# Moving VectorE's two-input chores, the key copy and the side products within each pair of heads

## What is computed

```python
x = x + attn_a(_layernorm(x), ...)
x = x + ffn(_layernorm(x), ...)
x = x + attn_b(_layernorm(x), Wq, Wk, Wv, Wo, gamma, beta)
x = x + ffn(_layernorm(x), ...)

# attn_b, its input called x
q = jnp.einsum('bsd,hde->bhse', x, Wq)      # k and v likewise
scores = jnp.einsum('bhse,bhte->bhst', q, k)
attn = softmax(where(causal, scores / sqrt(E), -inf))
out = jnp.einsum('bhst,bhte->bhse', attn, v)
y = x + heads @ Wo
y = (y - mu) * rsqrt(var + LN_EPS) * gamma + beta

# ffn: M = 64, INNER = 16
s = jnp.einsum('btd,dm->btm', x, Win) + bin_
h = relu(s[..., None] * W1 + b1)
g = jnp.einsum('btmh,mh->btm', h, W2) + b2
out = jnp.einsum('btm,md->btd', g, Wout) + bout
```

## Time and profile before

| | |
|---|---|
| median of 3 runs | 909.11 us (909.02 to 909.72) |
| the profiled execution | 910.46 us, its span 908.7 us |
| PE busy | 732.3 us (81%) |
| DVE busy | 740.5 us (81%) |
| ACT busy | 542.1 us (60%) |
| POOL busy | 522.9 us (58%) |
| heads | from about 239 us; the last pair's maxima at 864 us |

### The profile page before, as it was taken

The page is one execution under the profiler, slowest core; times in us unless marked ns, Lnnn a source line. Parts: engine busy times, 40 slices in busy tenths (PEclk is TensorE's granted clock), DMA queues, the critical chain, the costliest instruction groups (busy, mean ns, idle before and its releaser), DMA issues. The chain is left out here.

```text
span 908.7 us, 21242 instructions
## 1 busy us (share of the span) xinstructions
PE 732.3 (81%) x7592; PEld 524.5 (58%) x7592; DVE 740.5 (81%) x1422; ACT 542.1 (60%) x1511; POOL 522.9 (58%) x496
## 2 busy tenths in 40 slices
PE   3476666641899999998899899889989998998852
PEld 2365555531557676675677567666756665675541
DVE  1478888864577789889989988998898899899973
ACT  0357666652466665675677567666756666765643
POOL 2146666443165666756756575676658566656831
PEclk9598878855799999999999999999999999999995
DMA  9111110101199987897789688888878887887740
GB/s 202 42 32 42 50 56 35 36 35 46 21 144 155 155 141 132 140 149 124 127 138 152 108 141 132 142 131 138 151 117 131 144 139 125 136 154 126 133 93 22
DMA packets 367142, 100.29 MB, mean 110 GB/s; under 512 B 347968, under 2 KB 364864, under 8 KB 367040
## 3 DMA queue, kind: packets, MB, share of 16 engines
q1 hardware_dynamic: 363776, 96.86, 61.6%
q10 hardware_dynamic: 3264, 2.10, 0.9%
HBM read 8.73 MB, written 2.10 MB: 12 GB/s over the span
## 5 line engine op out<-in xcount | busy, mean ns | idle before, releaser
L1018 POOL TENSOR_TENSOR prob_hl<-prob,prob_hl 128x768 f16<-128x768 f32 (+1 forms) x192 | 347.8, 1812 | 235.6 <-DVE prob_hl L957 235.6
L933 ACT ACTIVATE prob<-wide,neg_max 128x128 f32<-128x128 f32 (+3 forms) x512 | 264.5, 525 | 209.1 <-DVE neg_max L969 209.0
L969 DVE TENSOR_REDUCE neg_max<-wide 128x2 f32<-128x256 f32 (+3 forms) x256 | 203.6, 816 | 66.5 <-PE wide L847 65.0
L842 PE MATMUL wide<-k_sb,q_sb 64*128 64x128 f32 (+3 forms) x1024 | 190.8, 470 | 2.6 <-ACT prob L933 1.6
L867 PE MATMUL bank<-v_hi,prob_t 128*128 128x64 f16 x1280 | 132.2, 193 | 16.6 <-DMA prob_t<-prob_hl 8.8
L869 PE MATMUL bank<-v_hi,prob_t 128*128 128x64 f16 x1280 | 132.2, 193 | 0.0
L868 PE MATMUL bank<-v_lo,prob_t 128*128 128x64 f16 x1280 | 132.2, 193 | 0.0
L957 DVE CAST prob_hl<-prob 128x768 f16<-128x768 f32 (+1 forms) x192 | 126.4, 658 | 1.8 <-ACT prob L933 1.6
L867 PEld LDWEIGHTS bank<-v_hi,prob_t 128*128 128x128 f16 x1280 | 115.5, 98 | 20.5 <-issue 10.6
L869 PEld LDWEIGHTS bank<-v_hi,prob_t 128*128 128x128 f16 x1280 | 114.0, 98 | 0.0
L868 PEld LDWEIGHTS bank<-v_lo,prob_t 128*128 128x128 f16 x1280 | 113.8, 98 | 0.0
(11 more groups left out here) (190 smaller groups left out, 1474.6 us busy)
## 6 DMA issues: line engine op xcount, KB each, us to landing
prob_t<-prob_hl SPq DMA_TRANSPOSE x384, 3.1
x_next<-in_L_attn_a_in_features SPq DMA_DIRECT2D x8, 256.0 KB, 3.1
x_attn<-in_L_attn_a_in_features SPq DMA_DIRECT2D x8, 256.0 KB, 3.0
x_sb<-x_done SPq DMA_DIRECT2D x8, 256.0 KB, 2.3
y_res<-bn_y SPq DMA_DIRECT2D x8, 256.0 KB, 2.3
out_x<-x_done SPq DMA_DIRECT2D x8, 256.0 KB, 2.7
wq_a<-in_L_attn_a_w_q ACTq DMA_DIRECT2D x1, 512.0 KB, 5.3
wq_b<-in_L_attn_b_Wq SPq DMA_DIRECT2D x1, 512.0 KB, 8.3
```

The lines of the kernel that those rows point to most:

```text
L842: pe.matmul(dst[:, h, c:c + m], q[e, i * P:(i + 1) * P], k[e, 0:m], start=(i == UNIT_ROWS[u][0]), stop=False)
L933: last = act.activation(prob_2[s][:, at:at + m], score_banks(p, s)[:, h, c:c + m], ACT.Exp, bias=neg_max[p % 2][:, h, i:i + 1], accum_out= ...
L969: last = dve.tensor_reduce(neg_max[p % 2][:, :, i:i + 1], score_banks(p, s)[:, :, c:c + m], AX.X, ALU.max, negate=True)
L1018: pool.tensor_tensor(prob_hl[u][:, w:2 * w], prob_2[u][:, 0:w], prob_hl[u][:, 0:w], ALU.subtract)\
```

## The change

Five moves, with the same arithmetic:

1. The key copy goes from DVE (s = 1, after the cast) to ACT (s = 1, after the `ctx_t` copy).
2. The adds go from s = 0 (behind `v_lo`) to s = 1, between the maxima and the cast of unit 0, one pair later; the relus go one pair later too.
3. Centering and residual are done in one piece of four instructions each, at s = 2 of pairs 3 and 4, between the maxima of unit 2 and the cast of unit 1.
4. POOL's and DVE's later chores follow by a step: `ffn_xb`, roots and the applied norm about two units later, statistics and moments one unit later.
5. PE's side products come last in a pair, behind `values_tensor`, and one pair later (turn in pair 7, Win in pair 0, Wout in pair 1; for sequence 6 one pair later in the drain). ACT's copies of their results move behind the exponentials and `v_hi`. There is one drain body more.

```diff
-        DRAIN = 2 * HP + 2
+        DRAIN = 2 * HP + 3
...
-        def unit_of_ffn(b, p, s):
-
-            if b == B:
-                return p * NU + s if p < NU else None
-            return p if s == 0 and 0 <= b - 2 < B else None
+        def relu_at(b, p, s):
+
+            if b == B and p > 0:
+                k = (p - 1) * NU + s
+                return (B - 2, k) if k < J else None
+            c, j = (b - 2, p - 1) if p > 0 else (b - 3, J - 1)
+            return (c, j) if s == 0 and 0 <= c < B and c != B - 2 else None
+
+        def adds_at(b, p, s):
+
+            found = []
+            c, j = (b - 2, p - 2) if p > 1 else (b - 3, J - 2 + p)
+            if s == 1 and 0 <= c < B and c != B - 2:
+                found.append((c, j))
+            k = (p - 1) * NU + s
+            if b == B and 0 < k <= J:
+                found.append((B - 2, k - 1))
+            return found
...
-        def keys_vector(dve, b, p):
+        def keys_scalar(act, b, p):
             n = number(b, p)
-            wait(dve, "k_ps", n + 1)
-            wait(dve, "s2", n - 1)
-            dve.tensor_copy(k_sb[p % 2][:, :], QK).then_inc(sem("k_sb"), 1)
+            wait(act, "k_ps", n + 1)
+            wait(act, "s2", n - 1)
+            act.copy(k_sb[p % 2][:, :], QK).then_inc(sem("k_sb"), 1)
...
-                if s == 2 and p == 6 and 0 <= b - 1 < B:
+                if s == 2 and b < B - 1:
+                    values_tensor(pe, b, p)
+                if s == 2 and p == 7 and 0 <= b - 1 < B:
                     back_turn_tensor(pe, b - 1)
-                if s == 2 and p == 7 and 0 <= b - 1 < B:
-                    back_s_tensor(pe, b - 1)
+                if s == 2 and p == 0 and 0 <= b - 2 < B:
+                    back_s_tensor(pe, b - 2)
                 if s == 2 and leaves(b, p) is not None:
                     back_out_tensor(pe, leaves(b, p))
-                if s == 2 and b < B - 1:
-                    values_tensor(pe, b, p)
...
+                for c, j in adds_at(b, p, s):
+                    back_add_vector(dve, c, j)
+                if s == 2 and p == 3 and 0 <= b - 1 < B:
+                    back_center_vector(dve, b - 1)
+                if s == 2 and p == 4 and 0 <= b - 1 < B:
+                    back_residual_vector(dve, b - 1)
                 u = (s - 1) % NU
                 if pair_exists(*(before if s == 0 else (b, p))):
                     split_vector(dve, *(before if s == 0 else (b, p)), u)
...
-                if s == 1 and pair_exists(*later(b, p)):
-                    keys_vector(dve, *later(b, p))
-                back_adds_vector(dve, b, p, s)
...
         def back_out_tensor(pe, c):
             wait(pe, "g_add", J * c + J)
+            wait(pe, "g_done", c)
```

More of the change, by code:

```diff
@@ L803, in project_tensor @@
             wait(pe, *(("k_sb", n) if done == "q_ps" else ("q_sb", n + 1)))
-            if done == "q_ps" and p == 0:
+            if done == "q_ps" and p == 1:
                 wait(pe, "g_xt", b - 1)
-            if done == "q_ps" and p == 1:
+            if done == "q_ps" and p == 2:
                 wait(pe, "g_s", b - 1)
-            if done == "q_ps" and p == 2:
+            if done == "q_ps" and p == 3:
                 wait(pe, "g_done", b - 2)
@@ L943, in heads_scalar @@
                     act.copy(ctx_t[:, :], MB[:, :]).then_inc(sem("ctx_t"), 1)
+                if s == 1 and pair_exists(*later(b, p)):
+                    keys_scalar(act, *later(b, p))
                 if s == 2 and b < B - 1:
                     values_scalar(act, b + 1, p, MB)
-                j = unit_of_ffn(b, p, s)
-                if j is not None and j < J:
-                    back_relu_scalar(act, b - 2, j)
+                if s == 2 and p == 7 and 0 <= b - 1 < B:
+                    back_xt_scalar(act, b - 1)
+                if s == 2 and p == 0 and 0 <= b - 2 < B:
+                    back_s_scalar(act, b - 2)
+                if relu_at(b, p, s) is not None:
+                    back_relu_scalar(act, *relu_at(b, p, s))
         def split_vector(dve, b, p, u):
@@ L1068, in back_rstd_gpsimd, with back_center_vector @@
                 .then_inc(sem(f"{done}_rstd"), 1)
-        def back_center_vector(dve, c, half):
+        def back_center_vector(dve, c):
             wait(dve, "gy_mv", c + 1)
-            for i in range(half * QB // 2, (half + 1) * QB // 2):
+            for i in range(QB):
                 last = dve.scalar_tensor_tensor(out=y_gb[:, i, :], in0=y_res[:, c * QB + i, :],
@@ L1076, in back_center_vector, with back_residual_vector @@
             last.then_inc(sem("g_c"), 1)
-        def back_residual_vector(dve, c, half):
-            wait(dve, "g_c", 2 * c + 2)
+        def back_residual_vector(dve, c):
+            wait(dve, "g_c", c + 1)
             wait(dve, "gy_rstd", c + 1)
             wait(dve, "x_beta", c + 1)
-            wait(dve, "g_xb", c)
-            for i in range(half * QB // 2, (half + 1) * QB // 2):
+            wait(dve, "g_y", 2 * c)
+            for i in range(QB):
                 last = dve.scalar_tensor_tensor(out=x_ffn[:, i, :], in0=y_gb[:, i, :],
@@ L1125, in back_gpsimd @@
                 wait(pool, "kept", 16 * B)
-                wait(pool, "g_x", 2 * c)
+                wait(pool, "g_x", c)
                 pool.tensor_tensor(x_beta[:, :, :], x_sb[:, seq(c), :],
@@ L1131, in back_gpsimd @@
                 back_rstd_gpsimd(pool, y_norm, "gy", c)
-            if p == 4 and u == 2:
-                wait(pool, "g_x", 2 * c + 2)
+            if p == 5 and u == 0:
+                wait(pool, "g_x", c + 1)
                 wait(pool, "g_done", c - 1)
@@ L1137, in back_gpsimd @@
                     .then_inc(sem("g_xb"), 1)
-            if p == 5 and u == 0:
+            if p == 5 and u == 2:
                 back_rstd_gpsimd(pool, ffn_norm, "gf", c)
@@ L1141, in back_gpsimd @@
                     .then_inc(sem("gf_nm"), 1)
-            if p == 5 and u > 0:
-                if u == 1:
+            if p == 6 and u < 2:
+                if u == 0:
                     wait(pool, "gf_rstd", c + 1)
@@ L1146, in back_gpsimd @@
                     wait(pool, "g_xt_ps", c)
-                for i in range((u - 1) * QB // 2, u * QB // 2):
+                for i in range(u * QB // 2, (u + 1) * QB // 2):
                     last = pool.tensor_scalar(ffn_norm.y[:, i, :], x_ffn[:, i, :], ffn_norm.neg_mean[:, i:i + 1],
@@ L1256, in _ @@
             queries_scalar(act, 0, 0)
+            keys_scalar(act, 0, 0)
             over_pairs(act, heads_scalar)
```

34 lines of the change are left out of this document (8 added, 26 removed).

## The result

The changed kernel takes 882.59 us in the median of four runs (878.94 to 884.83), the kernel before 909.07 beside it (908.64 to 909.72): ratio 0.9704, 95% interval 0.9671 to 0.9738, 26.5 us less. The prediction was 877. The profiled execution is the fastest of the four, 878.94 us, its span 877.1.

A forecast was written before the change was run, and what follows sets the result against it. PE sets the pace in bare heads; with chores it waits for DVE, held behind GpSimd's subtractions. Savings of 34.8 us less 3.0 in the drain, net 32 from profiled 910.46, less 1.35 to the median, gave 877 us; range 865 to 893.

The forecast's parts named there:

- PE as the new bound: Full sequences: DVE ceases to be the bound; 80.96 us falls to PE's floor of 73.75 plus 2.0, 75.75.
- The adds: At s = 1, behind unit 0's maxima: 0.74 us instead of 1.58, at least 0.84 saved a pair; pushed-back work has slack.
- key copy off DVE: -0.60 us a pair: Key copy moved to ACT in each pair: DVE saves 0.60 us, and ACT's copy costs 0.
- Pairs 3 to 7: Late casts of unit 2 delay `ctx_sb`; PE waits 0.1 us in pair 3, 0.3 to 0.4 in the others.
- late transposes hold PE a little everywhere: Rival: queueing transposes make PE wait 0.35 us in each of 56 pairs, 897 us; chance 12%.
- Centering and residual: Pairs 3 and 4, in one piece at t = 7.6: 1.2 us each instead of 3.6 and some 2.2.
- GpSimd's root holds them: Rival: in pair 3 centering stands still for two root instructions, 1.2 us later, 8.4 in seven sequences, 885 us; chance 7%.
- Sequence 7: Pair 0 to pair 7: transfers become the floor at 8.3 us a pair, 67.15 falls to 60.7, -6.4 us.
- The drain: Kernel's end: sequence 6's adds start later, 0.8 us of waiting and 2.2 for three more adds, 3.0 us given back.
- nothing happens: Rival: adds stand still in their new place too, pairs keep their pitch, 909 us; chance 3%.
- late transposes of unit 0 make it slower: Rival: unit 0's low half lands late, PE waits 1.2 us in 48 pairs, 58 us, 935 us; chance 3%.
- everything fits: Rival: no wait in pairs 3 to 7, 12 us less than the forecast, 865 us; chance 4%.

The follow-up runs named there:

- spread: Changed kernel with centering and residual as two instructions each at s = 1 and s = 2, GpSimd's applied norm one instruction a unit: 883.14 us, ratio 0.9706.
- light_low: Changed kernel, but from sequence 2 on a low half's transpose moves only two blocks, with as many transposes issued: 876.72 us, ratio 0.9637.
- second measurement: The changed kernel run once more, unedited, to see where its executions differ: 880.56 us, ratio 0.9676.

## Why the prediction was right, and where not

**PE as the new bound: right.** PE is busy for 74.70 of 75.80 us, before for 75.29 of 80.90. A full sequence takes 75.9 us in the mean of four; I gave 75.75. But what lies between it and the floor of 73.75 was right in size and wrong in place, as the paragraph on pairs 3 to 7 says; that the two sums agree to 0.2 us is in part luck. My sign "pitches of 8.9 to 9.5 in every pair" holds for pairs 2 to 6 only: those that hold a product took 10.18, 9.88 and 9.74.

**The adds: right.** 0.74 us each in the pairs of the row above, a mean of 0.849 over all 56, 1.563 before. Not every one is free of GpSimd: in pair 7 of four sequences the add takes 1.09 to 1.36, and in sequence 7, where PE leaves less room, one takes 1.69 (at 790.35, beside a subtraction of 789.35 to 791.49) and one 1.94; one of the drain takes 2.17. Slack was predicted for what they push back, and it held: no more than 1.1 us of PE's 75.80 is idle. The run with the adds put back gave 902.89 against an expected 902.

**Key copy: a term put down as DVE's saving that PE never sees.** The step "key copy off DVE: -0.60 us a pair" was true for DVE and nearly without effect, at most 2.6 us of 26 to 29. My sum did not rest on it, as it went by PE's floor; but my reading that ACT's copy costs nothing held only because other moves put the maxima on time. In the kernel before it costs 11 us.

**Pairs 3 to 7: the size right, the step wrong.** I had "`ctx_sb` then ends at about t = 3.7 of the next pair [...] So PE waits about 0.4 us". The casts of unit 2 do stand still (1.43 to 1.85 us), but PE's wait is for the landing of what they and the subtraction behind them deliver. I had worked out the slack of unit 0's low half only. The case in rows, pairs 6 and 7 of sequence 3: on DVE the late cast,

```profile
513.07 1.64 DVE L971 CAST prob_hl<-prob 128x1024 f16<-128x1024 f32 x1
```

on SP's queue the issue of its low half and of the next unit's high half,

```profile
517.01 1.23 SPq L1049 DMA_TRANSPOSE prob_t<-prob_hl  x1
518.34 2.55 SPq L1046 DMA_TRANSPOSE prob_t<-prob_hl  x1
```

and on PE the weighted values that wait:

```profile
521.76 0.19 PE L880 MATMUL bank<-v_hi,prob_t 128*128 128x64 f16 x1 [0.65 <-DMA prob_t<-prob_hl]
```

Two things add up here: the cast is 0.96 us late, and the transfer of 517.01 lands 4.6 us after its issue, where the median is 3.2. My slack had the median landing, and counted from the subtraction's end.

Fourteen such waits make 8.8 us, some 1.3 for each of seven sequences. "I am wrong if PE waits for transposes", the prediction says, and by that sign this step failed. What the four sequences 3 to 6 (303.6 us) hold above PE's own work can be read from where its scores begin. From the scores of one unit to those of the next a bare pair takes 3.55 + 2.80 + 2.58 = 8.93 us, and pair 2 of sequence 4 takes just that. The products add 0.90, 0.86 and 0.45, so a sequence is 73.65 us of PE's work: the floor of 73.75 was right. Of the 9.0 us above it, 5.0 lie in units in which PE waits for `prob_t`, 0.9 in those with a wait for `ctx_t`, 0.8 in those with one for ACT's `x_attn`, and 2.4 in units with no wait shown. With the lighter transfers the first fall to 0.4 and the others rise from 4.0 to 6.3: most of what is won at one wait comes back at the next. So the rival "late transposes hold PE a little everywhere" is right in kind, and far off in size: not 0.35 us in each pair but 1.3 a sequence.

**Centering and residual: right.** 1.13 us for the four in pair 3. The rival in which GpSimd's root holds them is out: the root runs from 568.62 to 569.78, beside centerings that run from 568.14 to 569.27, and their four take 1.13 us. The 1.19 of the earlier trace rows were beside a root too; the four residuals behind them, of the same form, took 1.12 (884.79) while GpSimd was idle. The root takes 1.16 here instead of 1.02, but not by the centerings: beside them it took 1.02 in rows 9, and again in pair 3 of sequence 1 of the changed kernel (342.34). A cast runs beside its end where it took 1.16; that the cast is the reason is not shown, as in the `spread` kernel one beside its start (570.52) left it at 1.02. The blocking rule that I cited, of the Trainium skill (SBUF — State Buffer, Who interferes with whom), holds in these traces for the long subtractions and not for this short instruction.

**Sequence 7: mis-sized.** -3.8 and -3.9 us measured, -6.4 predicted. The step that failed is "the transfers become the floor: share 0.83 over 80.00 us and 8 pairs is 8.3 us of transfers a pair": a mean share is no duration, and with the share at 0.52 the sequence takes hardly less, 63.07 us. By my terms PE's work from pair 0 to pair 7 was 7 x 8.0 and 1.8 for two products, 57.8 us; it is busy for 60.11 of 63.00 and idle for 2.9. Pitches by DVE's maxima (9.46, 9.39, 8.83, 8.90, 9.11, 9.08 and 8.57) hide PE's pace here, since the maxima are up to 1.2 us late. From scores to scores PE does pair 2, which has no wait, in 784.69 - 776.54 = 8.15 us, where I had 8.0, and pairs 4 and 5 in 9.33 and 9.91, with waits for `prob_t` of 0.93, 0.98 and 0.45 us in them:

```profile
776.54 0.93 PE L855 MATMUL wide<-k_sb,q_sb 64*128 64x128 f32 x8
784.69 0.93 PE L855 MATMUL wide<-k_sb,q_sb 64*128 64x128 f32 x8
...
804.67 0.19 PE L880 MATMUL bank<-v_hi,prob_t 128*128 128x64 f16 x1 [0.98 <-DMA prob_t<-prob_hl]
```

What I had not counted is the time of SP's issues:

```profile
791.57 2.26 SPq L1049 DMA_TRANSPOSE prob_t<-prob_hl  x1
793.88 0.57 SPq L1054 DMA_DIRECT2D out_x<-x_done  x1
794.56 1.24 SPq L1046 DMA_TRANSPOSE prob_t<-prob_hl  x1
795.89 1.23 SPq L1049 DMA_TRANSPOSE prob_t<-prob_hl  x1
```

The long issue begins when the subtraction of 789.35 to 791.49 ends, which is late because GpSimd's `x_beta` (787.66, 1.74 us) stood ahead of it. From 794.56 to 815.20 SP then issues transposes without a pause of over 0.2 us, 1.33 from one start to the next, so six of them need 8.0 us of PE's 8.15, and what is late stays late: the low half whose subtraction ends at 800.13 is issued at 801.24, lands 3.3 us later, and PE has waited 0.98 us for it. `light_low` has as many issues and so does not test them. Why some issues take 2.3 us stays open, and no run has fewer or shorter ones.

**The drain: right within 0.6 us.** +3.6 and +3.4 measured, +3.0 predicted. The rows of the changed kernel's DVE that answer to the earlier trace rows (the last maxima are at 829.10, before at 864.26):

```profile
843.54 0.55 DVE L1106 TENSOR_SCALAR ffn_g<-relu_two,w,b 128x512 f32<-128x512 f32 x1 [1.32 <-PE bank L1175]
...
846.98 0.68 DVE L1061 TENSOR_TENSOR y_res<-bank,y_res 128x512 f32<-128x512 f32 x1
847.58 0.74 DVE L1110 SCALAR_TENSOR_TENSOR ffn_g<-relu_two,w,ffn_g 128x512 f32<-128x512 f32 x1
...
849.02 0.73 DVE L1110 SCALAR_TENSOR_TENSOR ffn_g<-relu_two,w,ffn_g 128x512 f32<-128x512 f32 x1
...
849.96 1.60 DVE L1110 SCALAR_TENSOR_TENSOR ffn_g<-relu_two,w,ffn_g 128x512 f32<-128x512 f32 x2
...
854.33 0.86 DVE L1066 BATCH_NORM_STATS2 fn_stats<-x_ffn 128x6 f32<-128x128 f32 x4
```

The sum `y_res` comes 17.88 us after the last maxima (16.25 before): 1.6 us, where I had 0.8 for the first add's wait for the product with Wout (it ends at 843.54); that all of the 1.6 is this wait is argued, not shown. From there to the last statistics it is 7.35 us (5.44 before): 1.9 for three more adds, where I had 2.2.

**The forecast against the median.** The terms sum to -34.8 + 3.0 = -31.8 by the prediction. By the table the heads gave 32.4 and 30.8 us and the drain took back 3.6 and 3.4, net 28.8 and 27.4. So the terms were 3.0 to 4.4 us too good, 2.5 or 2.6 of it in sequence 7. The profiled execution still came out at 878.94, beside the sum's 878.5, because its front was 2.8 us shorter, by no doing of the change. And I had taken the median to lie 1.35 us below the profiled execution, as before; here it lies 3.65 above it. In the second measurement it is 880.56.

**The rivals that are out:** that nothing happens (0.74 us an add), that the root holds the centering, that late transposes of unit 0 make it slower (no wait over 1.3 us for a transpose, 14 in all), and that everything fits (75.9, not 73.75, us a sequence).

## What to carry to other kernels

Put an engine's two-input instructions directly ahead of the instruction for which GpSimd waits: there they are cheap, and the delay falls on work that has slack, as long as the pace leaves GpSimd time to be done (in sequence 7 two of seven adds took over 1.6 us again). Count what a move is worth from the bound that is left, not from the busy time it frees; and where several moves serve one aim, expect each alone to bring little and each undone to cost most, since any late instruction is enough. A copy handed to an idle engine also moves the moment at which its bank comes free, and those who write into that bank next pay for it.

## What the runs showed of the hardware

A root on POOL of four elements a partition didn't hold centerings beside it (1.13 us for four, beside a root of 1.16), nor did centerings alone lengthen a root (1.02 us). Where four adds ran beside POOL's short chores, it was POOL that stood still: instructions of 0.20 us took 0.61 and 0.66, and the applied norm 2.23 instead of 1.74, while the adds took 3.30 us, 0.82 each, as three in a row do in the drain of the kernel before (2.46). On SP's queue the issue of a transpose takes 1.23 us, at times 2.55; six a pair at a distance of 1.33 fill 8.0 us, whatever the transfers' share shows. And taking a large part of the low halves' transfers away (share 0.92 to 0.52 in sequence 7) changed PE's pace by less than 1%; the number of issues stayed the same.
